# Second and third layer: the scores of sixteen heads in one visit of four 32-row tiles, and the steps of a round in a new order

## The reference

```python
def attention(q, k, v, mask):                 # 16 heads, DK = 16
    s = einsum('bqhd,bkhd->bhqk', q, k) / sqrt(16)
    s = where(masked, very_negative, s)       # 2nd layer: a mask per sequence, both attentions
    p = softmax(s, axis=-1)                   # 3rd layer: one mask, first attention only
    return einsum('bhqk,bkhd->bqhd', p, v)

x = norm1(x + attention(x wq, x wk, x wv, mask1) wo)
x = norm2(x + attention(x wq2, context wk2, context wv2, mask2) wo2)
x = norm3(x + relu(x w1 + b1) w2 + b2)        # 256 -> 1024 -> 256
```

## Time and profile before

| what | value |
|---|---|
| median of 3 runs | 3744.31 us (3732.96 to 3747.83) |
| the profiled execution's own time | 3738.52 us |
| its span in the trace | 3736.8 us |
| TensorE busy | 3314.4 us, 89% |
| VectorE (DVE), ScalarE (ACT), GpSimd (POOL) busy | 2052.0, 1931.9, 1686.7 us |
| mean granted TensorE clock | 0.954 of full |

### The profile page before, as it was taken

How to read it: one execution, slowest core, us unless ns; L and a number is a source line. 1 busy time by engine, 2 the same in 40 slices (tenths; PEclk the granted TensorE clock), 3 DMA queues, 4 the chain that set the end, 5 groups by cost and what they waited for, 6 DMA issues and landing times. The chain is left out here.

```text
span 3736.8 us, 77616 instructions
## 1 busy us (share of the span) xinstructions
PE 3314.4 (89%) x26224; PEld 2677.5 (72%) x26224; DVE 2052.0 (55%) x4094; ACT 1931.9 (52%) x7894; POOL 1686.7 (45%) x2020
## 2 busy tenths in 40 slices
PE   8999996889999997499999999748999999976887
PEld 5988894688888887267777777626777777754664
DVE  3455553444444443356666666535666666744665
ACT  2444442333434333266666666426666666634775
POOL 1223221034344445235666666623565665662444
PEclk9999998999999999699999999969999999997999
DMA  3111113110111110311111111021111111102331
GB/s 112 48 46 65 62 34 119 52 36 19 45 48 48 48 45 32 108 55 47 58 49 58 60 53 52 21 101 47 48 52 56 41 54 56 41 29 94 98 97 54
DMA packets 192550, 213.56 MB, mean 57 GB/s; under 512 B 30208, under 2 KB 161536, under 8 KB 189696
## 3 DMA queue, kind: packets, MB, share of 16 engines
q1 hardware_dynamic: 192384, 211.40, 17.6%
HBM read 131.59 MB, written 58.72 MB: 51 GB/s over the span
## 5 line engine op out<-in xcount | busy, mean ns | idle before, releaser
L1514 ACT ACTIVATE third_stage<-third_psum,third_neg_max 128x128 f32<-128x128 f32 x1024 | 363.2, 387 | 27.1 <-DVE third_neg_max L1490 26.6
L1514 ACT ACTIVATE second_stage<-second_psum,second_neg_max 128x128 f32<-128x128 f32 x1024 | 363.2, 387 | 23.4 <-DVE second_neg_max L1490 21.9
L1496 DVE COPY second_stage<-second_psum 128x512 f32<-128x512 f32 x256 | 175.6, 686 | 134.4 <-PE second_psum L1449 133.6
L1496 DVE COPY third_stage<-third_psum 128x512 f32<-128x512 f32 x256 | 175.6, 686 | 122.9 <-PE third_psum L1449 122.2
L1514 ACT ACTIVATION_READ_ACCUMULATOR second_stage<-second_psum,second_neg_max 128x1 f32 x1024 | 232.3, 227 | 0.0
L1514 ACT ACTIVATION_READ_ACCUMULATOR third_stage<-third_psum,third_neg_max 128x1 f32 x1024 | 232.3, 227 | 0.0
L1490 DVE TENSOR_REDUCE second_neg_max<-second_psum 128x4 f32<-128x512 f32 x256 | 175.0, 684 | 102.2 <-PE second_psum L1438 102.0
L1490 DVE TENSOR_REDUCE third_neg_max<-third_psum 128x4 f32<-128x512 f32 x256 | 174.9, 684 | 85.3 <-PE third_psum L1438 85.3
L534 POOL TENSOR_TENSOR cross_ff_hidden_lo<-cross_ff_relu,cross_ff_hidden_hi 128x256 fp32r<-128x256 f32 x128 | 93.3, 730 | 283.4 <-DVE cross_ff_hidden_hi L529 283.4
L1514 ACT ACTIVATE fourth_stage<-fourth_psum,fourth_neg_max 128x128 f32<-128x128 f32 x512 | 182.2, 387 | 3.5 <-DVE fourth_neg_max L1490 3.5
L1449 PE MATMUL third_psum<-third_eye,third_stage 128*128 128x128 f32 x1024 | 156.6, 276 | 6.2 <-DVE third_stage L1496 5.8
(11 more groups left out here) (432 smaller groups left out, 12443.4 us busy)
## 6 DMA issues: line engine op xcount, KB each, us to landing
second_stage<-second_a_k SPq DMA_DIRECT2D x512, 16.0 KB, 1.8
third_stage<-third_a_k SPq DMA_DIRECT2D x512, 16.0 KB, 1.8
cross_arena<-in_l0b_packed SPq DMA_DIRECT2D x6, 1024.0 KB, 4.9
self_arena<-in_l0a_packed SPq DMA_DIRECT2D x4, 1024.0 KB, 6.2
self_x_raw<-in_x_t SPq DMA_DIRECT2D x8, 512.0 KB, 3.8
self_x_rows<-in_x_rows SPq DMA_DIRECT2D x8, 512.0 KB, 3.8
self_ct_raw<-in_ctx_t SPq DMA_DIRECT2D x8, 512.0 KB, 4.4
context_hi<-self_ct_hi SPq DMA_DIRECT2D x8, 512.0 KB, 5.0
```

Of the source, the lines that this page charges most:

```text
L1496: dve.tensor_copy(self.sh.p_turned[:, h % 4, :, :], psum[:, TURN_BANK, :].rearrange("p (x k) -> p x k", x=4)) \
L1514: ins = act.activation(self.sh.p[:, h % 4, x, :], psum[:, SCORE_BANKS[h % 4], x * SEQ:(x + 1) * SEQ], ACT.Exp, bias=self.sh.neg_max[:, h % ...
```

## The change

`AttendWide` replaces `Attend16` in both attentions of the two layers. A visit of `pe_scores` now handles a whole batch. The keys stand in blocks of two heads (`k_block` is half as wide), and for each half c of the features four matmuls of 32 rows and 256 columns go to the four score banks, so a group's bank holds two heads of each half. The four masks come first, in one stretch. All four banks are claimed together. `pe_mix` is one visit of 16 matmuls a batch instead of two of 8. The number of exponentials, maxima, transposes, products and DMAs stays as it is.

The order of the steps is rewritten on every engine. A round is now four sections, which are called x0, x1, y0 and y1 here. Each starts with `start(before, after)`, the scores of the batch after and the mix of the batch before, and goes on with the four turns of the batch between, with other steps among them.

```diff
+class AttendWide(Attend16):
+    visits = B2
+    def pe_scores(self, pe, r, banks, b):
...
+        banks.claim(pe, r, *SCORE_BANKS)
...
+        for c in range(C):
+            for t, bank in enumerate(SCORE_BANKS):
+                rows = slice(32 * t, 32 * t + 32)
+                ins = pe.matmul(banks.psum[:, bank, c * T2:(c + 1) * T2].rearrange("p (e k) -> p e k", e=2),
+                                self.proj.q[rows, c, tokens], self.proj.k_block[rows, c, :, tokens],
+                                start=self.mask is None, stop=self.mask is None or c == C - 1)
...
+        def steps(r, ok):
+            turn = [(att1, r, 0, ok(0)), (att1, r, 1, ok(0)),
+                    (att2, Back(r, 1), 0, ok(-1)), (att2, Back(r, 1), 1, ok(-1))]
+            first = (att2, Back(r, 2), 1, ok(-2))
+            last = (att1, Back(r, -1), 0, ok(1))
+            around = [first] + turn + [last]
+            return [[a[:3] if a[3] else None for a in around[i:i + 3]] for i in range(4)]
```

TensorE, the first section of `body(r)` after the change:

```diff
+                start(x0[0], x0[2])
+                turn(x0[1], 0)
+                if ok(-3):
+                    ff.pe_hidden(pe, Back(r, 3), banks, 4)
+                    ff.pe_out(pe, Back(r, 3), banks, 2, norm3.sum_ready)
+                turn(x0[1], 1)
...
+                    proj2.pe_q(pe, Back(r, 1), banks, norm1.yt)
+                turn(x0[1], 2)
...
+                    proj2.pe_v(pe, Back(r, 1), banks, ct)
+                turn(x0[1], 3)
...
+                    att2.pe_out(pe, Back(r, 2), banks, norm2.sum_ready)
```

More of the change, by code:

```diff
@@ L2015, in _ @@
                 body(r)
-            for r in range(LAST - 1, END + 1):
+            for r in range(LAST - 1, END):
                 body(r)
@@ L2064, in body, with exp, spread, hi @@
+            def exp(after, t):
+                if after:
+                    att, n, b = after
+                    att.act_exp(act, n, psum, b, t)
+            def spread(before):
+                if before:
+                    att, n, b = before
+                    att.act_spread(act, n, psum, b)
+            def hi(before):
+                if before:
+                    att, n, b = before
+                    att.act_hi(act, n, b)
             def body(r):
                 ok = exists(r)
-                steps(r, ok, True)
@@ L2067, in body @@
-                steps(r, ok, False)
+                (x0, _, x0_next), (x1, _, x1_next), (y0, _, y0_next), (y1, _, y1_next) = steps(r, ok)
+                if ok(-4):
+                    norm3.act(act, Back(r, 4), psum)
+                exp(x0_next, 0)
+                spread(x0)
+                if ok(-3):
+                    ff.act_relu(act, Back(r, 3), psum, 4)
+                hi(x0)
+                exp(x0_next, 1)
+                if ok(-1):
+                    proj2.act_q(act, Back(r, 1), psum)
@@ L2069, in _ @@
+                if ok(-2):
+                    ff.act_relu(act, Back(r, 2), psum, 2)
+                hi(y1)
+                exp(y1_next, 2)
+                if ok(0):
+                    norm1.act(act, r, psum)
+                exp(y1_next, 3)
             act.wait_ge(layer.lo_made.sem, layer.slots)
@@ L2174, in make_flags, with inverse, lo @@
                     m.pool(pool, r, att.scores_ready)
+            def inverse(here):
+                if here:
+                    att, n, b = here
+                    att.pool_inverse(pool, n, b)
+            def lo(before):
+                if before:
+                    att, n, b = before
+                    att.pool_lo(pool, n, b)
             def body(r):
                 ok = exists(r)
-                first, second = Back(r, 1), Back(r, 2)
+                x0, x1, y0, y1 = steps(r, ok)
+                inverse(x0[1])
+                if ok(0):
+                    layer.pool_residual(pool, r, norm1.sum_ready)
+                if ok(-3):
+                    norm2.pool_rows(pool, Back(r, 3), (norm3.sum_ready, 0))
+                lo(x0[0])
+                if ok(-3):
+                    ff.pool_lo(pool, Back(r, 3), 4)
@@ L2214, in body @@
                 if ok(0):
                     make_flags(mask[1], att2, r)
+                    norm1.pool_hat(pool, r)
+                inverse(y1[1])
+                lo(y1[0])
                 if ok(-2):
-                    norm2.pool_rows(pool, second, (norm3.sum_ready, 0))
-            for m, att in zip(mask, (att1, att2)):
-                if m is not None and m.per_batch and att is att1:
-                    m.pool(pool, 0)
+                    ff.pool_lo(pool, Back(r, 2), 2)
+            if mask[0] is not None and mask[0].per_batch:
+                mask[0].pool(pool, 0)
@@ L2281, in body, with start, turn @@
+            def start(before, after):
+                if after:
+                    att, n, b = after
+                    att.pe_scores(pe, n, banks, b)
+                if before:
+                    att, n, b = before
+                    att.pe_mix(pe, n, banks, b)
+            def turn(here, t):
+                if here:
+                    att, n, b = here
+                    att.pe_turn(pe, n, banks, b, t)
             def body(r):
@@ new lines, in body @@
+                turn(x1[1], 1)
+                if ok(-3):
+                    ff.pe_out(pe, Back(r, 3), banks, 4, norm3.sum_ready)
+                    ff.pe_hidden(pe, Back(r, 3), banks, 6)
+                turn(x1[1], 2)
+                if ok(-3):
+                    ff.pe_out(pe, Back(r, 3), banks, 5, norm3.sum_ready)
+                if ok(-2):
+                    norm2.pe(pe, Back(r, 2), banks)
+                turn(x1[1], 3)
+                start(y0[0], y0[2])
+                turn(y0[1], 0)
@@ new lines, in body @@
+                if ok(1):
+                    proj1.pe_q(pe, Back(r, -1), banks, xt)
+                if ok(-3):
+                    ff.pe_out(pe, Back(r, 3), banks, 6, norm3.sum_ready)
+                turn(y0[1], 1)
+                if ok(-2):
+                    ff.pe_hidden(pe, Back(r, 2), banks, 0)
+                if ok(-3):
+                    ff.pe_out(pe, Back(r, 3), banks, 7, norm3.sum_ready)
+                turn(y0[1], 2)
+                if ok(1):
+                    proj1.pe_v(pe, Back(r, -1), banks, xt)
@@ new lines, in body @@
+                turn(y0[1], 3)
+                if ok(0):
+                    att1.pe_out(pe, r, banks, norm1.sum_ready)
+                start(y1[0], y1[2])
+                turn(y1[1], 0)
+                if ok(-2):
+                    ff.pe_out(pe, Back(r, 2), banks, 0, norm3.sum_ready)
+                if ok(0):
+                    pe.wait_ge(layer.ct_loaded.sem, layer.ct_loaded.at(r, 32))
+                    proj2.pe_k(pe, r, banks, ct)
+                turn(y1[1], 1)
+                if ok(-2):
+                    ff.pe_out(pe, Back(r, 2), banks, 1, norm3.sum_ready)
+                    ff.pe_hidden(pe, Back(r, 2), banks, 2)
@@ L2288, in _ @@
+                turn(y1[1], 2)
+                if ok(0):
+                    norm1.pe(pe, r, banks)
+                turn(y1[1], 3)
+                if ok(-3):
+                    norm3.pe(pe, Back(r, 3), banks)
             pe.wait_ge(layer.lo_made.sem, 1)
```

410 lines of the change are left out of this document (218 added, 192 removed).

## The result

| | before | after |
|---|---|---|
| median | 3741.19 us (3732.96 to 3747.83, 4 runs) | 3875.69 us (3864.77 to 3883.13, 4 runs) |
| ratio | | 1.0358, 95% interval 1.0324 to 1.0392 |
| span of the profiled execution | 3736.8 us | 3876.0 us |
| mean granted TensorE clock | 0.954 | 0.927 |

What follows compares the result with a forecast made beforehand. TensorE, busy 51.4 of 52.0 us a steady round, was taken as the bound. From 3738.5 us, +11 for steady rounds, -18 at layer ends and +2 for the tail gave 3734, so a 3739 us median; range 3660 to 3805.

Steps and rivals of the forecast that it cites:

- y0: Section y0 of a steady round: forecast 13.1 us, with waits at EV_BANK, for 12.2 us of TensorE work.
- 24 steady rounds: Steady rounds of both layers: 52.7 us against 52.0 and 50.9 against 50.7, +11 us in all.
- ends of the layers: Fill taken as even, within 10 us; each layer's end -9, together -18; +2 for a longer tail.
- The clock: TensorE's clock in the waits: a fall called no rival of weight, waits being 2 us at most; no chance given.
- TensorE's own work: TensorE in a steady round: 45.0 us instead of 52.0; score block 1.08, mix 1.01, masks 0.95.
- rival of pairs: Scores on TensorE: 32-row tiles run only two at a time, 3.4 us a round more, 3850 us; chance 0.10.
- The waits: TensorE waits for exponentials, norm1 and EV_BANK: some 7.5 us of each round's gain turn into waits.
- rival of a late DVE queue: Section y1: norm1's hat or DVE's queue comes late, 1 to 2 us a round, about 3790 us; chance 0.15.
- The Trainium skill's rule: PSUM read-outs: tiling doesn't speed evacuation; by busy time a round takes 45.0 us, by read-out order 52.7.
- T1: Theory after the result: waits as forecast, 52.7 us a round; clock falls after most, what follows runs at half speed.
- T2: Theory after the result: border waits come from single banks and ScalarE's order, not tile form; without them the new order wins.

Runs made afterwards that it cites:

- e2: Changed kernel plus unread matmuls in TensorE's waits: nine before y0's masks, eight before norm3, three before x0's masks; 3838.14 us, ratio 1.0257.
- e7: Changed kernel with each mask claiming only its own bank, norm1's POOL rows behind the batch's low part, v and norm1's columns in MIX_BANK; 3759.23 us, ratio 1.0054.
- e10: e7 plus six unread matmuls ahead of y0's masks or scores and six ahead of x0's; 3697.49 us, ratio 0.9892.
- e5: Changed kernel with POOL's rows of norm1 moved behind the batch's low part at the start of y0; 3864.74 us, ratio 1.0343.
- e9: e7 with relu 6 and norm1's columns behind exp 3, norm2's columns in MIX_BANK, VectorE's splits behind the second maximum; 3690.20 us, ratio 0.9883.
- e6: Changed kernel with v of both attentions and norm1's columns turned into MIX_BANK instead of EV_BANK; 3810.09 us, ratio 1.0206.
- e3: Changed kernel with each mask matmul claiming only its own score bank instead of all four together; 3827.20 us, ratio 1.0227.

## Why the prediction was wrong, point by point

- **How far off, and where.** The sum gave 3734 us for the profiled execution, which took 3877.7: 144 more. 65 of them lie in the 24 steady rounds (+11 forecast, +76 measured), 69 at the ends of the layers (-18 and +2 forecast, +53 measured), and 10 ahead of the second layer. Three steps failed.
- **The clock** is the step that had the mechanism wrong: "A fall of the clock is no rival of weight: the waits are 2 us at most, and the fourth layer, with TensorE busy 178.8 of 200, keeps the clock at 1.00". The waits were indeed 2 us, and the clock fell to 0.50 after most of them. The row that should have warned was in hand: at the end of the second layer, with waits, the clock stood at 0.89. The fourth layer's mean of 200 us says how much TensorE idles, not how long at a time or behind what work. The price in the changed kernel is 1.9 us a round in the second layer, 0.6 or more in the third, and 38 us in all (e2); in e7 it is 1.3 and 3.0 us a round (e10).
- **TensorE's own work** was right: score block 1.08 forecast and 1.07 measured, mix 1.01 and 1.02, masks 0.95 and 0.97. Row tiles of 32 run four at a time, so the rival of pairs (0.10) is out.
- **The waits** were right in place, cause and size: 2.0 before the masks of y0, 1.6 before norm3 and 0.67 behind it. At full clock three of four sections came within 0.2 us of the forecast in both layers (e2).
- **y0** was mis-sized: 13.1 forecast and 14.0 measured at full clock in the second layer, and in the third 12.2 and 14.0, from its own first score to the first mask of y1 (the 15.0 above holds these masks too). The sum lets the first maximum start 0.12 behind the scores, so it takes VectorE's queue for free, and says of POOL only that it "gives no wait". It gives none to TensorE. It lengthens a neighbour's work on VectorE from 1.1 to 3.2 us, ahead of the first maximum. Without that (e5), rounds at full clock have a y0 of 13.6 and 12.6, so 0.4 to 0.5 remain. The rival of a late DVE queue (0.15) was the right kind, but in y0 and not in y1. The row that should have warned was in hand here too. The third layer of the kernel before has a long split in each of its twelve steady rounds, beside the same two row operations of POOL (1.28 and 1.34 us long, from 2877.44 on), at a place where it held nobody up:

```profile
2877.89 1.11 DVE L1646 CAST third_n_yt_hi<-third_n_y 128x512 fp32r<-128x512 f32 x1
2879.04 1.65 DVE L1648 TENSOR_TENSOR third_n_yt_lo<-third_n_y,third_n_yt_hi 128x512 fp32r<-128x512 f32 x1
```

- **Ends of the layers**: "I take the fill as even" and -9 at each end, together -18; measured +23.4, +19.2 ahead of the steady rounds and +3.7, +6.6 behind. In the second layer the first scores come 5.7 us later after the layer's start (45.6 against 39.9). The trace has 5.2 of them as a longer wait for the key DMAs: 12.87 us before the first mask, until the 16th lands, against 7.71, until the eighth. Most of the rest went when the waits went: in e9 the fill of the second layer is 192.2 us, 3 over the 189.2 of before, where the changed kernel has 212.6. The drain's gain did not come, in e9 neither (123.9 us from the window's end to the last VectorE operation of the second layer, against 120.3 before). The clock is at 0.83 in the changed kernel's last 80 us; what else sets the drain was not tested and stays open.
- **The Trainium skill's rule** (TensorEngine Tiling (Array Packing), PSUM Bottleneck) that tiling speeds up TensorE but not the evacuation of PSUM agrees with the trace: in the twelve rounds of the second layer TensorE's busy time fell from 617 to 588 us and ScalarE's stayed at 414 (414.7 and 414.4). It bites here as the prediction read it, as a rule on the order of read-outs and not on their busy time: by bank and order alone, with the same 414 us of ScalarE work, e6 gives back 3.4 us a round in the second layer, and e9, with the edits of e3, e5 and e6, 6.6. These figures hold the clock's part.

So T1 holds, with y0 as an addition and with the open point that not every wait brings the clock down. T2 holds: e9, in the new order and with the new tiles, is faster than the kernel before.

## What to carry to other kernels

A faster operation on an engine that is 99% busy opens waits, so forecast the longest gap and not only their sum: here a gap of 2 us behind transposes cost its length and in three of four cases more, since what followed ran at half the clock. If one visit takes every score bank, the next begins only when the last reader is done; claim bank by bank, put into a bank that stands empty what would wait for a busy one, and move behind the last reader what no one needs before it. To learn what the clock costs, fill the wait with matmuls that nobody reads: if the kernel gets faster, it was the clock.

## What the runs showed of the hardware that was not expected

- The granted clock fell from 1.00 to 0.50 behind single waits of 2.0 us that followed transposes, with TensorE at work at the full clock before them: behind 18 of 24 such waits in the changed kernel. Length alone does not decide. In the second layer of e6 the clock fell behind only 5 of 24 waits of 2.0 and 2.6 us, and in the third behind all twelve of 2.6 us. Waits of 1.0 us left it alone in e9, but in five of twelve rounds of e2's third layer it fell behind one of 1.0 us at a turn and one of 0.6 to 0.8 us at the product behind it. What else decides stays open. Waits filled with unread matmuls left it at 1.00 (e2's second layer, e10).
- VectorE's cast of 128x512 from fp32 to its high half took 0.36 to 0.43 us alone and 1.55 beside POOL's row operations, and the subtraction 0.69 and 1.64. Two maxima over PSUM banks took 1.29 us beside such an operation (2942.03 in the changed kernel) and 1.27 alone. The Trainium skill, SBUF — State Buffer, SBUF: two separate sides, says that VectorE and GpSimd share a pair of SBUF ports under a lock, which one holds for its whole instruction; of VectorE's operations it names those in a two-port mode and those with two SBUF inputs. The trace agrees in which operations get longer: the two that read and write SBUF, and not the maxima, whose source is a PSUM bank.
